# Two layer-norm statistics of an RWKV block taken apart: row sums on VectorE, sums of squares on ScalarE

## The reference, cut to what matters

```python
h = _layernorm(x, axis=-1) * (1 + ca) + sa          # norm A, then scale and shift
...                                                  # _L0_attn_ref(h):
h = _layer_norm(x, ln1_g, ln1_b)                     # norm 1, of norm A's result
hh = _time_shift(h)
k = (h * tm_mk + hh * (1 - tm_mk)) @ Wk.T            # v and r likewise
wkv = _wkv_run(k, v, tm_first, tm_decay)
x = x + jax.nn.sigmoid(r) * wkv @ Wo.T
h = _layer_norm(x, ln2_g, ln2_b)                     # norm 2
...                                                  # channel mixing, experts
def _layer_norm(x, g, b):
    m = jnp.mean(x, axis=-1, keepdims=True)
    v = jnp.mean((x - m) ** 2, axis=-1, keepdims=True)
    return (x - m) * jax.lax.rsqrt(v + EPS) * g + b
```

## Time and profile before

| | |
|---|---|
| Median of 3 runs | 931.16 us |
| The runs | 930.25, 931.16, 931.88 us |
| The profiled execution | 931.54 us |
| Its span, first to last instruction | 929.7 us |
| PE busy | 886.9 us (95%) |
| DVE busy | 519.2 us (56%) |
| ACT busy | 382.6 us (41%) |
| POOL busy | 381.3 us (41%) |

### The profile page before, as it was taken

How to read it: one execution, slowest core, us unless ns; L and a number is a source line. 1 busy time by engine, 2 the same in 40 slices (tenths; PEclk the granted TensorE clock), 3 DMA queues, 4 the chain that set the end, 5 groups by cost and what they waited for, 6 DMA issues and landing times.

```text
span 929.7 us, 13549 instructions
## 1 busy us (share of the span) xinstructions
PE 886.9 (95%) x4264; PEld 715.3 (77%) x4265; DVE 519.2 (56%) x995; ACT 382.6 (41%) x632; POOL 381.3 (41%) x282
## 2 busy tenths in 40 slices
PE   6899879999998999999999999999999999999796
PEld 2467768788776888888888888888887888888675
DVE  5796989986847111454145614561695444444388
ACT  2656564674745433322232123225433333333342
POOL 3321300100022546126203520359447599897464
PEclk9999989999999999999999999999999999999998
DMA  9678477663255328395215321566345789776677
GB/s 354 215 223 274 157 242 226 192 205 117 65 177 209 113 92 278 118 295 192 91 53 163 102 80 57 163 223 215 125 138 187 249 264 269 241 269 229 199 248 182
DMA packets 122400, 174.07 MB, mean 187 GB/s; under 512 B 8792, under 2 KB 70232, under 8 KB 119280
## 3 DMA queue, kind: packets, MB, share of 16 engines
q1 hardware_dynamic: 59472, 111.58, 35.4%
q0 software_dynamic: 9216, 34.61, 12.2%
q10 hardware_dynamic: 53664, 27.26, 10.2%
HBM read 97.60 MB, written 75.83 MB: 187 GB/s over the span
## 4 chain that ended last, share of the span: by engine, by line
PE 80%; DVE 9%; issue 3%; DMA 3%; ACT 3%; another core or an unknown queue 1%; POOL 1%; SPq 0%; DVEq 0%; ACTq 0%; POOLq 0%
PE kk_ps L426 6%; PE kv_ps L426 6%; PE kk_ps L428 6%; PE kv_ps L428 6%; PE kk_ps L427 6%; PE kv_ps L427 6%; PE mm_ps L426 5%; PE mm_ps L428 5%; PE mm_ps L427 5%; PE up_ps L426 4%; PE up_ps L428 3%; PE up_ps L427 3%; PE dn_ps L426 3%; PE dn_ps L428 3%; PE dn_ps L427 3%
## 5 line engine op out<-in xcount | busy, mean ns | idle before, releaser
L1573 DVE TENSOR_TENSOR silu<-kk_ps,silu 128x512 fp32r<-128x512 f32 x64 | 44.3, 691 | 198.8 <-ACT silu L2241 193.8
L2237 ACT ACTIVATE kk_ps<-kk_ps 128x512 f32<-128x512 f32 x64 | 37.2, 582 | 207.0 <-PE kk_ps L428 200.4
L426 PE MATMUL kk_ps<-xk,cm_w 128*128 128x512 f32 x256 | 100.8, 394 | 0.0
L426 PE MATMUL kv_ps<-cm_w,silu 128*128 128x512 f32 x256 | 100.5, 393 | 0.0
L428 PE MATMUL kk_ps<-xk,cm_w 128*128 128x512 f32 x256 | 99.8, 390 | 0.0
L428 PE MATMUL kv_ps<-cm_w,silu 128*128 128x512 f32 x256 | 99.7, 390 | 0.0
L427 PE MATMUL kk_ps<-xk,cm_w 128*128 128x512 f32 x256 | 99.6, 389 | 0.0
L427 PE MATMUL kv_ps<-cm_w,silu 128*128 128x512 f32 x256 | 99.6, 389 | 0.0
L2407 POOL TENSOR_TENSOR cm_w<-stage,cm_w 128x1024 fp32r<-128x1024 f32 x16 | 38.7, 2423 | 90.7 <-ACT cm_w L2023 74.9
L1900 DVE TENSOR_TENSOR xsT<-xs_ps,xsT 128x512 fp32r<-128x512 f32 x42 | 28.9, 691 | 76.8 <-ACT xsT L2324 74.1
L2465 POOL TENSOR_TENSOR rs<-mv,neghalf 128x1 f32<-128x1 f32 x16 | 16.1, 1008 | 127.4 <-DVE mv L1598 127.4
(11 more groups left out here) (298 smaller groups left out, 2328.4 us busy)
## 6 DMA issues: line engine op xcount, KB each, us to landing
xs_s<-zero ACTq DMA_DIRECT2D x13, 1024.0 KB, 6.9
ys_s<-zero ACTq DMA_DIRECT2D x13, 1024.0 KB, 6.3
xsb<-xs_s SPq DMA_DIRECT2D x44, 256.0 KB
ys_s<-ysb SPq DMA_DIRECT2D x41, 256.0 KB
ex_raw<-in_wex POOLq DMA_DIRECT2D x9, 1024.0 KB
stage<-in_wcm SPq DMA_DIRECT2D x16, 512.0 KB, 3.9
wmod<-in_wmod SPq DMA_DIRECT2D x6, 1024.0 KB, 10.8
ex_raw<-in_wex SPq DMA_DIRECT2D x6, 1024.0 KB, 6.9
```

The source lines that it names most:

```text
L426: pe.matmul(out, lhs[0], rhs[0], start=first, stop=False)
L1573: dve.tensor_tensor(silu[:, g % NSILU, 1, :], kk_ps[g % 2][:, :], silu[:, g % NSILU, 0, :].bitcast(F32), ALU.subtract).then_inc(s_silo, 1)
L2237: act.activation(kk_ps[g % 2][:, :], kk_ps[g % 2][:, :], ACT.Silu).then_inc(s_silu, 1)
```

## The change

Norm 1 and norm 2 (but for the last batch's norm 2) lose their `bn_stats` and `bn_aggr`. The instruction that writes the tile (`first_norm_c` for `xb`, `o_out` for `x2b`) now also writes the row's sum into `mv[:, j, 0]`. A new ACT function `squares` computes (sum - 512 x)^2 of each element and adds these up along the row into `mv[:, j, 1]`; what it writes beside the sum goes to buffers that are free then (`raw`, `rec`). A new DVE function `variance` scales the four sums of a batch and adds EPS in one small instruction. The rest (`rsqrt`, `centred`, `hn_out`) stays, with a factor of -1/512 in `centred`.

Moved in DVE's list: the closing of norm 2 (`variance(2)`) from the end of the body into the middle of the next body's `first_norm_a`; the closing of norm 1 from behind the statistics to behind `wkv(b, 0)`; `centred(1)` two instructions down; in the last body `centred(2)` behind R's first two blocks; `o_out` of the fourth tile ahead of V's last low part. In POOL's list the low parts of halves 8 and 9 move from batch 0, ahead of norm 2's `rsqrt`, to batch 1, behind norm 1's.

The diff, cut to its core:

```diff
                 for j in range(TT):
+                    if b >= 2 and j == 2:
+                        variance(2, b - 2)
                     dve.wait_ge(s_x[j], 16 * (b + 1))
                     own.up(dve.bn_stats(st1[:, j], xb[:, j]))
...
-                                             op0=ALU.mult, op1=ALU.add).then_inc(s_h0, 1)
-
-            def first_norm_d(b):
-                if b:
-                    dve.wait_ge(s_rs2, b)
-                for j in range(TT):
-                    dve.wait_ge(s_h0, b * TT + j + 1)
-                    own.up(dve.bn_stats(st2[:, j], xb[:, j]))
-                dve.wait_ge(s_dve, own.n)
-                aggregated(st2, mv2, s_st2)
+                                             op0=ALU.mult, op1=ALU.add, accum_out=mv2[:, j, 0:1]).then_inc(s_h0, 1)
+
+            def variance(kind, b):
+
+                mv, s_in, s_out = (mv2, s_sq2, s_st2) if kind == 1 else (mv3, s_sq3, s_st3)
+                dve.wait_ge(s_in, (b + 1) * TT)
+                dve.tensor_scalar(mv[:, :, 1:2], mv[:, :, 1:2], 1.0 / H ** 3, EPS, ALU.mult, ALU.add).then_inc(s_out, 1)
...
-                dve.tensor_tensor(x2b[:, j], mm_ps[j][:, :], x2b[:, j], ALU.add).then_inc(s_x2, 1)
...
+                if b + 1 < NB:
+                    dve.scalar_tensor_tensor(out=x2b[:, j], in0=mm_ps[j][:, :], scalar=1.0, in1=x2b[:, j],
+                                             op0=ALU.mult, op1=ALU.add, accum_out=mv3[:, j, 0:1]).then_inc(s_x2, 1)
...
                 wkv(b, 0)
+                if more:
+                    variance(1, b + 1)
                 mixed("R", b, 3)
+                v_out(b, 1)
+                mixed_lo("R", b, 2)
                 if more:
                     centred(1, b + 1)
-                v_out(b, 1)
-                mixed_lo("R", b, 2)
                 wkv(b, 1)
...
+            def squares(kind, b, tiles=range(TT)):
+
+                for j in tiles:
+                    n = b * TT + j
+                    s_in, src, out, mv, s_sq = ((s_h0, xb, raw, mv2, s_sq2) if kind == 1 else
+                                                (s_x2, x2b, rec, mv3, s_sq3))
+                    act.wait_ge(s_in, n + 1)
+                    if kind == 1 and b >= 3 and j < 2:
+                        act.wait_ge(s_xkst[j], 32 * (b - 2))
+                    if n >= 2:
+                        act.wait_ge(s_sq, n - 1)
+                    act.activation(out[:, j % 2], src[:, j], ACT.Square, scale=-float(H), bias=mv[:, j, 0:1],
+                                   accum_out=mv[:, j, 1:2]).then_inc(s_sq, 1)
...
                 mixed_hi("R", b, [0, 1])
+                if more:
+                    squares(1, b + 1)
...
-                    mixed_hi("V", b + 1)
+                    mixed_hi("V", b + 1, [0, 1])
+                    squares(2, b, [0])
+                    mixed_hi("V", b + 1, [2])
+                    squares(2, b, [1])
+                    mixed_hi("V", b + 1, [3])
+                    squares(2, b, [2, 3])
...
-                for n in {0: (6, 7, 8, 9), NB - 1: (10, 11)}.get(b, ()):
+                for n in {0: (6, 7), 1: (8, 9), NB - 1: (10, 11)}.get(b, ()):
                     weight_lo(n)
```

More of the change, by code:

```diff
@@ L136, in adaln_block @@
         rs1 = sbuf(ph1, "rs1", [P, TT])
-        st2 = sbuf(ph1, "st2", [P, TT, 6])
         mv2 = sbuf(ph1, "mv2", [P, TT, 2])
@@ L294, in adaln_block @@
         s_st2 = sem("s_st2")
+        s_sq2 = sem("s_sq2")
+        s_sq3 = sem("s_sq3")
         s_rs2 = sem("s_rs2")
@@ L1335, in centred @@
                     dve.wait_ge(s_hn, hn_count(kind, b - 1, TT - 1))
-                dve.scalar_tensor_tensor(out=nm[:, :].rearrange("p (t a) -> p t a", a=1), in0=mv[:, :, 0:1], scalar=-1.0,
+                dve.scalar_tensor_tensor(out=nm[:, :].rearrange("p (t a) -> p t a", a=1), in0=mv[:, :, 0:1],
+                                         scalar=-1.0 / H,
                                          in1=rs[:, :].rearrange("p (t a) -> p t a", a=1),
@@ L1395, in o_out, with last_stats @@
                 dve.wait_ge(s_h0r[j], 16 * (b + 1))
-                dve.tensor_tensor(x2b[:, j], mm_ps[j][:, :], x2b[:, j], ALU.add).then_inc(s_x2, 1)
[L1398 to L1401, removed]
+                if b + 1 < NB:
+                    dve.scalar_tensor_tensor(out=x2b[:, j], in0=mm_ps[j][:, :], scalar=1.0, in1=x2b[:, j],
+                                             op0=ALU.mult, op1=ALU.add, accum_out=mv3[:, j, 0:1]).then_inc(s_x2, 1)
+                else:
+                    dve.tensor_tensor(x2b[:, j], mm_ps[j][:, :], x2b[:, j], ALU.add).then_inc(s_x2, 1)
+            def last_stats(j):
+                if j == 0:
+                    dve.wait_ge(s_rs3, NB - 1)
+                dve.wait_ge(s_x2, (NB - 1) * TT + j + 1)
                 own.up(dve.bn_stats(st3[:, j], x2b[:, j]))
-                if b == NB - 1 and j >= TT - 2:
+                if j >= TT - 2:
                     dve.wait_ge(s_dve, own.n)
                     aggregated(st3, mv3, s_st3, *((0, j + 1) if j == TT - 2 else (j, TT)))
-                elif j == TT - 1:
-                    dve.wait_ge(s_dve, own.n)
-                    aggregated(st3, mv3, s_st3)
             def centred_last(part):
@@ L1432, in _ @@
             first_norm_c(0)
-            first_norm_d(0)
+            variance(1, 0)
             centred(1, 0)
@@ L1456, in _ @@
                     first_norm_a(b + 1)
-                if b:
-                    centred(2, b - 1)
-                if more:
+                    if b:
+                        centred(2, b - 1)
                     first_norm_b(b + 1)
+                else:
+                    variance(2, b - 1)
                 mixed("R", b, 0)
@@ L1464, in _ @@
                     first_norm_c(b + 1)
-                    first_norm_d(b + 1)
+                else:
+                    centred(2, b - 1)
                 mixed_lo("R", b, 0)
@@ L1531, in _ @@
                     mixed_lo("V", b + 1, 0)
-                    o_stats(b, 0)
                     o_out(b, 1)
@@ L1535, in _ @@
                     mixed_lo("V", b + 1, 1)
-                    o_stats(b, 1)
                     o_out(b, 2)
@@ L1539, in _ @@
                     mixed_lo("V", b + 1, 2)
-                    o_stats(b, 2)
+                    o_out(b, 3)
                     mixed_lo("V", b + 1, 3)
-                    o_out(b, 3)
-                    o_stats(b, 3)
                 else:
@@ L1546, in _ @@
                     o_out(b, 1)
-                    o_stats(b, 0)
+                    last_stats(0)
                     o_out(b, 2)
-                    o_stats(b, 1)
-                    o_stats(b, 2)
+                    last_stats(1)
+                    last_stats(2)
                     o_out(b, 3)
             centred_last(0)
-            o_stats(NB - 1, 3)
+            last_stats(3)
             centred_last(1)
@@ L2119, in _ @@
             weight_hi(1)
+            squares(1, 0)
             for i in range(2):
```

## The result

The changed kernel took 922.85 us, median of 6 runs (918.89 to 926.64), beside 931.23 for the kernel before (6 runs, 929.14 to 931.88): a ratio of 0.9921 with a 95% interval of 0.9893 to 0.9948. Two later measurements, each beside runs of before, gave 0.9948 (0.9924 to 0.9971) and 0.9954 (0.9933 to 0.9975), by the medians 4.6 and 5.0 us. Over all its runs after has 30, median 924.4, and before 93, median 930.1: **5.7 us**. The sign and the mechanism were right, the size was not, and by the later runs part of the first 8.4 us is no effect of the change.

A forecast was written before the change was run, and what follows sets the result against it. PE was taken to bound the kernel, with DVE last ahead of its 6.97 us wait in batch 1. Gains of 3.6 us in batch 1 and 0.0 in batch 2, from 931.16, gave 927.6 us, range 925.4 to 930.6.

The forecast's parts named there:

- What bounded the kernel, and who would be next: PE busy 886.9 of 929.7 us; DVE last ahead of PE's 6.97 us wait in batch 1, ACT next.
- DVE's 2.99 us: Batch 1: norm 1's statistics, aggregates and EPS on DVE, ahead of R's first low part, removed by the change.
- about 4 us: What would be left of PE's 6.97 us wait for the first hT in batch 1.
- The square: Each ACT square with row sum, 128x512: taken at 0.80 us, bounds 0.61 to 0.83.
- The sums on DVE: Row sums added to DVE's writes of xb: 0.1 us each; o_out some 0.17 dearer with form and sum.
- the second half: Second half of norm 2's turn on PE, batch 1: start at 117.9 for 121.52, gain 3.6 us.
- Batch 2: Four squares fill ACT's free 2.98 us, first hT at 182.76 for 182.78: gain 0.0, bounds -0.1 to 0.55.
- The clock: Behind PE's big wait in batch 1, the 2.0 us lost at the lower clock level stay lost.
- A rule that lost: Half rate for DVE's sums on xb: some 2.2 us more, batch 1's gain 3.3 in place of 3.6.
- The low parts: POOL's two moved low parts delay DVE in batch 1 by 3.9 us, covered by 1.6 us before PE needs it.
- The sum and its range: Batch 1's 3.6 us plus batch 2's 0.0 give 927.6 us; range 925.4 to 930.6.
- more gain: Rival: PE's shorter wait keeps the upper clock, or squares cost 0.61; 5.1 to 5.6 us, about 925.8; chance 0.13.

The follow-up runs named there:

- g1: Changed kernel with norm 1's four squares made twice in a row, in batches 1 and 2; PE's waits there 6.22 us for 3.40 and 3.55 for 0.73.
- f1: Changed kernel with ACT's high parts of weight halves 8 and 9 moved behind batch 1's second to_hT; median 922.62 us, ratio 0.9942.

## Why the prediction was wrong

**What bounded the kernel, and who would be next: right.** DVE's 2.99 us went, DVE and POOL were no longer last, and ACT's list took over without idle time; g1 and f1 show that list as the chain, microsecond for microsecond. PE's wait of "about 4 us" is 3.40.

**The square: mis-sized, and a step that failed.** I took 0.80, near the high end, "because the sum must be written out after the last element". It costs 0.71: the sum is read out by an instruction of its own, 0.19 to 0.20 us, which starts 0.61 behind the square's start, and the next ACTIVATE starts 0.09 later, while it runs. Four squares took 2.82 instead of 3.2.

**The sums on DVE: mis-sized.** I took 0.1 each, and 0.17 for each `o_out` with its new form. They cost 0.01 to 0.02: V's last block was mixed about 0.5 us earlier than I counted. With two cheaper squares of norm 2 (0.2), ACT's list of batch 1 began 0.65 us earlier than in my count (the weights at 99.16, by the time from K, not 99.8). With the four squares behind R's high parts (0.4) the two sizes together make 1.0 of the 1.1 us by which batch 1 was off: the second half came 4.72 us earlier in place of 3.6.

**Batch 2: 0.4 in place of 0.0**, from the same squares (within the bounds given, -0.1 to 0.55).

**The clock: nearly right.** I kept its 2.0 us as lost. The stretch from the second half to the next turn takes 16.6 to 16.8 us in before, 15.9 to 17.3 in after, 16.4 in f1 with 1.86 us of waiting, and 14.77 in batch 2, at a granted clock of 1.00 (2.4 GHz). By the means 1.7 of 1.9 us of loss stay, with 1 us of scatter from trace to trace of one kernel.

**A rule that lost.** The Trainium skill (Vector Engine (DVE) Microarchitecture Reference, section 7, Points that are easy to get wrong) says that `scalar_tensor_tensor` with two non-bf16 SBUF sources runs at half rate, as no port is left for reading the accumulator. Here it starts every 0.67 us with a sum and 0.66 without, at 512 columns of fp32; the measurement decides, against the rule for this form.

**The low parts: covered, as said,** but the prediction did not see how much hangs on the order. Their move costs 2.6 us alone and gains 2.4 behind the norms' part. In after the lock cost DVE 3.5 us (2.09 for the 0.15 of `nm`, which was named, and 2.87 for the 1.28 of two `dT`, in place of `wkv`) where 3.9 was counted from the earlier trace rows; whether PE pays it depends on which DVE instruction stands there. The Trainium skill (SBUF — State Buffer, section Who interferes with whom) says that a DVE instruction with two SBUF inputs contends with a GpSimd instruction that reads SBUF; the trace agrees, with these numbers.

**The sum and its range: this is the step that failed.** 4.7 us in batch 1, 0.4 in batch 2 and, by the means, 0.3 of clock (-0.6 to 0.8 in single traces) are 5.4, where I had 3.6: the square at 0.80 for 0.71 and DVE's sums at 0.1 for 0.01 to 0.02 make 1.4 of the 1.8 us between them. The rival "more gain" named 5.1 to 5.6 us, but by the upper clock or squares of 0.61, and got a chance of 0.13; that its number fits is luck, as neither came true. The high price of the square had no row behind it, and I put it near the upper bound although the row with two pointers was 0.71. And the range was made of the terms of stage 1 alone. "Stages 2 and 3 not touched" holds, but an execution there can be 8 us longer than another (212.5 to 220.8 us), and three runs of before within 1.6 us didn't show it. The difference between the first medians, 8.4 us, is 2.7 more than that of all runs. The traces place such scatter at the start, at the end of stage 1 and in the last stage; where it lay in the timed runs is not shown.

## What to carry to other kernels

When one engine's work goes, walk the next engine's list instruction by instruction: here the list, with the measured prices put in, gives the start of the second half to 0.1 us (116.9 counted and 116.8 measured, both from the start of K in before), and a price without a row belongs in the middle of its bounds. Parts of such a change don't add up: one that is worth nothing or costs something alone (a move in POOL's queue, an earlier start) can be what lets another one pay. And before reading a small gain from two traces, cut both at the same points: where stages that no edit touches differ, the difference is the execution's and not the kernel's.

## What the runs showed of the hardware

- An ACTIVATE with a sum along the row is two instructions, 0.72 us and a read-out of 0.19; from start to start 0.71 for 128x512. On DVE the read-out is 0.08 us and all but hidden.
- POOL's gathers took 0.96 us, but in five of fourteen traces the 20th to 22nd took 2.77, 3.43 and 3.43, always the same three, and in two more the 25th took 2.87 and 2.97, with nothing edited near them.
- Some ten completion signals of PE were 0.5 to 4.3 us late in one execution of fourteen; the cause is open.
- After a wait of 1.86 us of PE (f1) the granted clock was 0.66 from 115 to 120 us, 1.00 ahead of it; the stretch behind it took 16.4 us for 14.8 in batch 2, where the clock was 1.00 throughout and the wait 1.12. With a wait of 3.55 us in batch 2 (g1) the clock fell there too, to 0.66 in 185 to 190 us.
